# The last stage of a fused attention and expert kernel: two to three batches combined inside the last expert steps, another activation table in those steps, scatters released row by row, the last batch in halves

## The reference, cut to what matters

```python
xn  = _layernorm(x)                          # x: 8 batches of 512 tokens, 256 features
s   = attention(xn)                          # gated linear attention, 16 heads, chunks of 128
      # ... inside, at its end:
      o = o * rsqrt(mean(o * o, -1) + 1e-06) * norm_weight
      s = o @ Wo.T
# expert choice, E = 8 experts, each takes k = 128 tokens of each batch
gating, idx = top_k(softmax(xn @ gate_w.T) by expert, k)
h   = silu(x_in @ w_gate) * (x_in @ w_up)    # x_in = xn[idx], hidden width 1024
ffn = zeros.at[idx].add(gating * (h @ w_down))
out = x + s * silu(ffn)
```

## Time and profile before

| | us |
|---|---|
| median of 3 runs | 856.28 (855.05 to 857.82) |
| the profiled execution | 854.44 |
| its span, first to last instruction | 852.7 |
| PE busy in the span | 787.4 (92%) |
| DVE / ACT / POOL busy | 546.2 / 500.4 / 416.0 |
| mean granted clock of PE | 0.957 |

### The profile page before, as it was taken

One profiled execution on the slowest core, in us unless ns is written; L12 is line 12 of the kernel. 1 busy time (PEld: TensorE's weight loads), 2 busy tenths in 40 slices (PEclk: granted clock), 3 DMA queues, 4 the chain that ended last, 5 costly groups with the idle time before them and its releaser, 6 DMA issues.

```text
span 852.7 us, 17337 instructions
## 1 busy us (share of the span) xinstructions
PE 787.4 (92%) x6412; PEld 679.1 (80%) x6412; DVE 546.2 (64%) x1027; ACT 500.4 (59%) x1150; POOL 416.0 (49%) x362
## 2 busy tenths in 40 slices
PE   7637999999999999999999999999999999999950
PEld 5425888888888888888888888888888888888840
DVE  6875765676665666666566666666567656556567
ACT  5694754665556655666566655665466555654432
POOL 7756544554354716463265525471455435470221
PEclk9955999999999999999999999999999999999985
DMA  8298997676557757676666757576667767662939
GB/s 274 91 287 230 294 345 190 165 198 174 173 146 188 173 199 155 162 194 190 165 147 198 202 155 156 168 173 211 155 161 199 185 162 222 172 133 90 292 77 294
DMA packets 137605, 160.85 MB, mean 189 GB/s; under 512 B 11824, under 2 KB 108592, under 8 KB 137520
## 3 DMA queue, kind: packets, MB, share of 16 engines
q1 hardware_dynamic: 124800, 142.91, 55.9%
q0 software_dynamic: 12288, 16.79, 11.9%
q10 hardware_dynamic: 432, 0.04, 0.0%
HBM read 117.48 MB, written 42.21 MB: 187 GB/s over the span
## 4 chain that ended last, share of the span: by engine, by line
PE 83%; DVE 4%; DMA 3%; SPq 2%; POOL 2%; ACT 1%; issue 1%; DVEq 0%; ACTq 0%; POOLq 0%
PE y_ps L1547 21%; PE g_ps L1518 21%; PE up_ps L1518 20%; PE m_ps L1407 4%; PE a_ps L1470 4%; PE o_ps L1506 3%; PE m_ps L1452 3%; PE m_ps L1425 2%; DMA qk_dram<-qk_r 2%; PE m_ps L1445 2%; PE o_ps L1495 1%; PE m_ps L1435 1%; DMA xg<-xn_dram,idx_all 1%; DVE e_row L1290 1%; PE m_ps L1417 1%
## 5 line engine op out<-in xcount | busy, mean ns | idle before, releaser
L1547 PE MATMUL y_ps<-w_r,hid_r 128*128 128x256 f32 x1536 | 204.6, 282 | 1.6 <-DVE hid_r L1371 1.6
L1518 PE MATMUL up_ps<-xgt,w_r 128*128 128x512 f32 x768 | 205.6, 403 | 0.0
L1518 PE MATMUL g_ps<-xgt,w_r 128*128 128x512 f32 x768 | 201.6, 398 | 0.5 <-DVE sg L1355 0.5
L1547 PEld LDWEIGHTS y_ps<-w_r,hid_r 128*128 128x128 f32 x1536 | 192.6, 190 | 2.8 <-DVE hid_r L1371 2.0
L1355 DVE SCALAR_TENSOR_TENSOR sg<-sg,g_ps 128x512 f32<-128x512 f32 x128 | 87.6, 685 | 164.8 <-ACT sg L1131 164.8
L830 POOL TENSOR_TENSOR w_r<-w_raw,w_r 128x768 fp32r<-128x768 f32 x64 | 122.7, 1918 | 108.0 <-ACT w_r L1049 107.6
L1518 PEld LDWEIGHTS up_ps<-xgt,w_r 128*128 128x128 f32 x768 | 138.8, 189 | 28.0
L1518 PEld LDWEIGHTS g_ps<-xgt,w_r 128*128 128x128 f32 x768 | 136.5, 190 | 24.0 <-DVE sg L1355 0.7
L1131 ACT ACTIVATE sg<-g_ps 128x512 f32<-128x512 f32 x128 | 76.5, 597 | 119.5 <-PE g_ps L1518 119.5
L856 POOL DMA_INDIRECT ffn_dram<-y_sb,idx_all x64 | 105.1, 1643 | 75.1 <-DVE y_sb L1277 59.3
L825 POOL TENSOR_SCALAR_AFFINE_SELECT lb_row<-lb_row 128x1024 f32<-128x1024 f32 x62 | 75.9, 1234 | 75.6 <-DMA lb_row<-lb_tiles 75.5
(11 more groups left out here) (246 smaller groups left out, 1014.8 us busy)
## 6 DMA issues: line engine op xcount, KB each, us to landing
lb_row<-lb_tiles SPq DMA_DIRECT2D x62, 512.0 KB, 4.3
w_raw<-w_experts SPq DMA_DIRECT2D x64, 384.0 KB, 3.6
qk_dram<-qk_r SPq DMA_DIRECT2D x32, 512.0 KB, 4.6
k_st<-qk_dram SPq DMA_DIRECT2D x96, 128.0 KB, 3.7
arena<-qk_dram SPq DMA_DIRECT2D x192, 64.0 KB, 3.0
x_all<-x SPq DMA_DIRECT2D x8, 512.0 KB, 9.5
xn_dram<-x_all SPq DMA_DIRECT2D x8, 512.0 KB, 5.6
e_row<-lb_tiles SPq DMA_DIRECT2D x64, 64.0 KB
```

The costliest lines, as they stand in the source:

```text
L1518: mm = pe.matmul(bank[:, :], w_r[:, m, a, at:at + P], xgt[:, b, k, half * 512:(half + 1) * 512], start=(j == 0 and k == 0), stop=(j == len ...
L1547: mm = pe.matmul(y_ps[:, j, :], hid_r[p][:, a, j * P:(j + 1) * P], w_r[:, m, b, DOWN:DOWN + D], start=(m == 0 and q == 0 and j % 2 == 0), ...
```

## The change

It touches the steps from 130 on and the end stage.

- `f_at` is a plain float32 tensor `w_plain` over the same memory as `w_r`; Silu works in place on it, and `g_of` is gone.
- From piece 123 on (`SILU`, step 131) ACT uses Silu itself on `g_ps`; L1355 is gone in those steps, DVE's product takes scalar 2.0, and PE's gate waits for `sg_done` instead of `t_done`.
- The inverse root comes from one Abs_reciprocal_sqrt instead of Ln and Exp, with two Newton steps (eight small operations) instead of one.
- ACT applies Silu to the batches 0 to 3 in the steps 132 to 135. By the table `EARLY`, DVE makes the four products of batch 0 in step 132, adds batch 0 and makes two products of batch 1 in step 133, the other two and the addition of batch 1 in step 134, and the products of batch 2 in step 135; all stand behind the low part of the step.
- SP fetches only x of the batches 0 to 3 in step 128. x of 4 to 7 and the attention's result of batch 7 move to step 134, behind `fetch_f(3)`. The stores of 0, 1 and 2 stand ahead of the late fetches, and that of 3 between the second and the third of them.
- In group 15 `gated` takes its first two rows when PE has finished those (`first_rows`), and each scatter waits for its own row alone.
- Batch 7 is fetched, put through Silu, combined and stored in two halves.

```diff
...
+    SILU = TS + 3 - AHEAD
+    EARLY = {TS + 4: ((0, range(TPB), False),), TS + 5: ((0, (), True), (1, (0, 1), False)),
+             TS + 6: ((1, (2, 3), True),), TS + 7: ((2, range(TPB), False),)}
...
+                def fetch_last():
+                    for h in range(2):
+                        rows = ffn_dram[(B - 1) * N + h * N // 2:(B - 1) * N + (h + 1) * N // 2, :]
+                        sp.dma_start(f_at[B - 1][:, h * 512:(h + 1) * 512].rearrange("p (t d) -> p t d", d=D),
+                                     rows.rearrange("(t p) d -> p t d", p=P)).then_inc((f_in[B - 1], last_half)[h], 16)
...
@@ -795,28 +814,37 @@
                         sp.wait_ge(inter_done, B * (TPB - 1))
                         sp.wait_ge(e_done, TS)
                         sp.wait_ge(m_done, order["x", E - 1, 3] + 1)
-                        for n in range(6):
-                            fetch_x(n)
-                        sp.wait_ge(av_done, NT)
-                        for n in range(6, B):
+                        for n in range(F_EARLY):
                             fetch_x(n)
                     if u == TS + 3:
-                        fetch_s(B - 1)
                         sp.wait_ge(scattered, 16 * TPB * (2 * E - 1))
                     if TS + 3 <= u < TS + 3 + F_EARLY:
                         sp.wait_ge(dn_done, XS - MI + (u - TS - 3) + 1)
                         fetch_f(u - TS - 3)
+                    if u == TS + 6:
+                        fetch_s(B - 1)
+                        sp.wait_ge(av_done, NT)
+                        for n in range(F_EARLY, B):
+                            fetch_x(n)
                     if u in (0, 2):
                         load_lb(u // 2 + 4)
                     if u >= FREE and u % 2 == 0 and (u + 4) // 2 < 2 * NT:
                         load_lb((u + 4) // 2)
+                for n in range(F_EARLY - 1):
+                    store_out(n)
                 sp.wait_ge(dn_done, XS)
                 for n in range(F_EARLY, B):
                     sp.wait_ge(last_out[n - F_EARLY], 16)
-                    fetch_f(n)
-                for n in range(B):
+                    if n < B - 1:
+                        fetch_f(n)
+                    else:
+                        fetch_last()
+                    if n == F_EARLY + 1:
+                        store_out(F_EARLY - 1)
+                for n in range(F_EARLY, B - 1):
                     store_out(n)
-                sp.wait_ge(o_out, 16 * B)
+                store_last()
+                sp.wait_ge(o_out, 16 * (B + 1))
...
                     e, half = n // HALVES, n % HALVES
-                    pool.wait_ge(y_read, 2 * n + 2)
+                    if n < 2 * E - 1:
+                        pool.wait_ge(y_read, 2 * n + 2)
                     if n == 0:
                         pool.wait_ge(zeroed, 16 * B)
                     for t in range(TPB):
                         b = half * TPB + t
+                        if n == 2 * E - 1:
+                            pool.wait_ge(y_read, 2 * n + t + 1)
...
+                def silu(f):
+                    act.wait_ge(f_in[f], 16)
+                    act.activation(f_at[f], f_at[f], ACT.Silu).then_inc(g2_done, 1)
...
-                        act.activation(sg[:, :], g_ps[:, :], ACT.Tanh, scale=0.5).then_inc(sg_done, 1)
+                        act.activation(sg[:, :], g_ps[:, :], ACT.Tanh if n < SILU else ACT.Silu, scale=0.5 if n < SILU else 1.0)\
+                           .then_inc(sg_done, 1)
                     if first:
                         evacuate(first)
                     if u % NG == 0 and NG <= u <= TS:
@@ -1159,17 +1195,15 @@
                         split(second)
                     if u == TS + 2:
                         act.wait_ge(r_step, 1)
-                        act.activation(ln_ms[:, :], ms[:, :], ACT.Ln).then_inc(r_step, 1)
-                        act.wait_ge(r_step, 2)
-                        act.activation(r0[:, :], ln_ms[:, :], ACT.Exp, scale=-0.5).then_inc(r_step, 1)
-                for f in range(B):
-                    act.wait_ge(f_in[f], 16)
-                    if f == F_EARLY + 2:
-                        for t in range(TPB):
-                            act.wait_ge(last_out[t], 16)
-                    elif f >= 2:
-                        act.wait_ge(o_done, f - 1 if f < F_EARLY + 2 else F_EARLY + 1)
-                    act.activation(g_of[f], f_at[f], ACT.Silu).then_inc(g2_done, 1)
+                        act.activation(r0[:, :], ms[:, :], ACT.Abs_reciprocal_sqrt).then_inc(r_step, 1)
+                    if TS + 4 <= u < TS + 4 + F_EARLY:
+                        silu(u - TS - 4)
+                for f in range(F_EARLY, B - 1):
+                    silu(f)
+                for h in range(2):
+                    act.wait_ge((f_in[B - 1], last_half)[h], 16)
+                    at = slice(h * 512, (h + 1) * 512)
+                    act.activation(f_at[B - 1][:, at], f_at[B - 1][:, at], ACT.Silu).then_inc(g2_done, 1)
...
                     e, half = n // HALVES, n % HALVES
-                    dve.wait_ge(dn_done, (n + 1) * MI)
+                    if n < 2 * E - 1:
+                        dve.wait_ge(dn_done, (n + 1) * MI)
                     if n == 0:
                         dve.wait_ge(zeroed, 16 * B)
                         dve.wait_ge(topk, TOP_STEPS + 2)
                     dve.wait_ge(scattered, 16 * TPB * n)
                     for t in range(TPB):
                         b = half * TPB + t
+                        if n == 2 * E - 1 and t % 2 == 0:
+                            dve.wait_ge((first_rows, dn_done)[t // 2], (1, (n + 1) * MI)[t // 2])
                         ins = dve.tensor_scalar(y_sb[:, t, :], y_ps[:, t, :], gate_all[:, e, b:b + 1], None, ALU.mult)
-                        if t % 2 == 1:
+                        if t % 2 == 1 or n == 2 * E - 1:
                             ins.then_inc(y_read, 1)
-                def combine(f):
-                    if f == 0:
-                        dve.wait_ge(x_in, 16 * B)
-                        dve.wait_ge(s_in, 16 * B)
-                    dve.wait_ge(g2_done, f + 1)
-                    g = g_of[f]
-                    for t in range(TPB):
+                def weigh(f, tiles, step):
+                    if f % F_EARLY == 0 and 0 in tiles:
+                        dve.wait_ge(x_in[f // F_EARLY], 16 * F_EARLY)
+                        dve.wait_ge(s_in[f // F_EARLY], 16 * F_EARLY)
+                    dve.wait_ge(g2_done, step)
+                    for t in tiles:
                         at = slice(t * D, (t + 1) * D)
                         tile = f * TPB + t
-                        ins = dve.scalar_tensor_tensor(out=g[:, at], in0=g[:, at], scalar=r1[:, tile:tile + 1],
+                        ins = dve.scalar_tensor_tensor(out=f_at[f][:, at], in0=f_at[f][:, at], scalar=r1[:, tile:tile + 1],
                                                        in1=s_at[f][:, at], op0=ALU.mult, op1=ALU.mult)
-                    ins.then_inc(c_step, 1)
-                    dve.wait_ge(c_step, f + 1)
-                    dve.tensor_tensor(x_at[f], g, x_at[f], ALU.add).then_inc(o_done, 1)
+                        if t % 2 == 1:
+                            ins.then_inc(c_step, 1)
+                def add_tokens(f, at=slice(0, TPB * D)):
+                    dve.wait_ge(c_step, 2 * f + at.stop // 512)
+                    dve.tensor_tensor(x_at[f][:, at], f_at[f][:, at], x_at[f][:, at], ALU.add).then_inc(o_done, 1)
...
+                    dve.wait_ge(r_step, 2)
+                    for k, r in enumerate((r0, r1)):
+                        at = 4 * k + 2
+                        if k:
+                            dve.wait_ge(r_step, at)
+                        dve.tensor_tensor(nw[:, :], r[:, :], r[:, :], ALU.mult).then_inc(r_step, 1)
+                        dve.wait_ge(r_step, at + 1)
+                        dve.tensor_tensor(nw[:, :], nw[:, :], ms[:, :], ALU.mult).then_inc(r_step, 1)
+                        dve.wait_ge(r_step, at + 2)
+                        dve.tensor_scalar(nw[:, :], nw[:, :], -0.5, 1.5, ALU.mult, ALU.add).then_inc(r_step, 1)
+                        dve.wait_ge(r_step, at + 3)
...
-                    if 0 <= n < XS:
+                    if 0 <= n < min(XS, SILU):
...
-                        dve.wait_ge(t_done, n + 1)
-                        dve.tensor_tensor(up_ps[n % 2][:, :], sg[:, :], up_ps[n % 2][:, :], ALU.mult).then_inc(h_done, 1)
+                        if n < SILU:
+                            dve.wait_ge(t_done, n + 1)
+                            dve.tensor_tensor(up_ps[n % 2][:, :], sg[:, :], up_ps[n % 2][:, :], ALU.mult).then_inc(h_done, 1)
+                        else:
+                            dve.wait_ge(sg_done, n + 1)
+                            dve.scalar_tensor_tensor(out=up_ps[n % 2][:, :], in0=sg[:, :], scalar=2.0, in1=up_ps[n % 2][:, :],
```

(39 more changed lines are left out.)

18 lines of the change are left out of this document (4 added, 14 removed).

## The result

The changed kernel takes 850.41 us (median of 5, 847.27 to 851.75) against 855.09 for the kernel before in the same runs: ratio 0.9941, 95% interval 0.9922 to 0.9960, so 4.7 us faster. In a later set of runs it was measured again, unaltered: 0.9947 (0.9931 to 0.9963).

What follows compares the result with a forecast made beforehand. PE bounds the kernel up to step 129, then DVE's chain and the transfers, ending nearly together. Root, earlier scatter, new chain (843.95) and last store (3.9) gave span 848.25, 4.45 less, median 851.8; range 849.8 to 854.9.

Steps and rivals of the forecast that it cites:

- Root and table: Step 130: new inverse root and Silu's table load let PE's gate start 0.63 earlier, bounds 0 to 0.73.
- Work inside the steps fits: Expert steps near the end: Silu and products fit, DVE's cycle 4.19 against 4.24, nothing to spare; costed at 0.
- first rival: Steps before the last down: first batch lands late, behind 807.0, losing up to 2.6, so 854.4; chance 0.15.
- First scatter: Group 15 on POOL: gated by rows, it starts at 822.6 instead of 824.60, 2.0 earlier.
- The new chain: End stage: scatter and fetch of batch 4 bind, its Silu ends 831.85, then DVE's batches end at 843.45.
- Batches 5 to 7: End stage: 5 and 6 just fit behind batch 4; 0.5 added for stores before their fetches, bounds 0 and 1.4.
- signs of being wrong: End of kernel: low part behind 820.5, first scatter of 2.6, idle DVE ahead of batches 5 and 6, or last store of 5.
- second rival: End stage: scatters and fetches slower than costed, chain ends 1.1 to 2 later, 852.9 to 853.3; chance 0.20.
- The last store: End of span: 256 KB on a nearly empty queue lands in 3.9, bounds 2.9 and 5.2.
- total of 4.45: Whole span: forecast gain of 4.45, ending at 848.25.
- Third rival: Steps from 131: Silu's table doesn't serve ACT's copies, two loads a step, 2.35 slower, 858.6; chance 0.05.
- Addition against scatter: Group 15: if DVE's addition of batch 2 stops POOL's first scatter in the middle, it costs 1.1.

## Why the prediction was right, point by point

- *Root and table*: 0.63 forecast, 0.75 measured (0.73 was my upper bound). The gate's 0.63 came back as said; the rest is in the step behind it, where gate to gate was 4.34 before and is 4.24 after. Two loads of 1.28, sg 0.01 behind the second. The Trainium skill (ScalarE: Activation LUTs, What ACT_TABLE_LOAD costs) has a drain as part of each switch; the trace shows none on either side of these loads.
- *Work inside the steps fits*: right. All products ended before the next one, and the first batch landed at 802.2, 6.2 behind the load (forecast 6.8 to 7.9). DVE's cycle was 3.98 where I had added up 4.19, so there is a slack of 0.26 that I put at nearly nothing. The first rival's mechanism is real; the fetch order decides on it.
- *First scatter*: 2.0 earlier forecast, 2.22 measured.
- *The new chain*: products of batch 4 forecast 33.6 behind the load, measured 33.63 and 34.38; the 0.75 of the second is the longer fetch of batch 4.
- *Batches 5 to 7*: mis-sized, and one of my own signs of being wrong appeared, idle DVE ahead of batches 5 and 6. I gave 0.5 for the transfers that share the engines; DVE waited 0.56 and 0.95 in the first profile, 0.89 and 0.63 in the second. From the products of batch 4 to the last addition I forecast 12.1, and both profiles have 13.3: 1.0 more in waits and 0.2 in DVE's own work. I had said that these batches "just fit" behind batch 4; in fact the fetch of 6, 6.8 instead of 4.3, binds the end. The second rival was right in part, by transfers and not by POOL (its first scatter took 1.55). Last addition forecast at 45.7, measured 46.97 and 47.73.
- *The last store*: mis-sized the other way. I took 3.9, measured 2.1. End forecast at 50.0, measured 49.49 and 50.28. These two errors, 1.3 and 1.8, happened to cancel. That the total of 4.45 is so close to the 4.7 measured is luck; the terms up to batch 4 were right by their mechanism.
- *Third rival*: wrong; no table is loaded behind 797.55, so copies and Silu run from one table. The Trainium skill (ScalarE: Activation LUTs, Table sets: the hidden batching unit) has copy in every set; the trace agrees.
- *Addition against scatter*: a scatter that starts under a running addition waits, 2.54 against 1.56. DVE's addition at 820.96 ran beside a scatter that had begun at 820.15, without waiting. By the Trainium skill (SBUF — State Buffer, SBUF: two separate sides) whichever starts second is blocked; the trace agrees in the first direction and not in the second.

## What to carry to other kernels

When the last stage is a chain over tiles, count the transfers as a resource with a capacity, as the engines: here 7 us of DVE work were taken away, and it paid, for about half of the gain, by stores leaving before the rush. The stores of batches 0 and 1 are enough for it as far as the ratios can tell: with those of 2 and 3 late nothing was lost. A step with no slack can still be filled, if the first input is in place; look for what stands ahead of its fetch on the issuing queue. And read profiles of two kernels from the first instruction that differs, since executions differed by 7 us ahead of it.

## What the runs showed that I had not expected

A store of 256 KB landed 2.1 after issue on a quiet queue, one of 512 KB in 2.8 to 2.9. An adding scatter of 128 rows of 1 KB, the first of its group, landed in 3.7 to 3.9, a writing one in 2.4, of which the instruction on POOL took 1.55 and 1.00. The same kernel's first touched instruction came between 796.0 and 802.8 in two profiles.
